# Softmax sums of the macaron block: their inverses stored to DRAM in the order of z, in 4-byte pieces

## The reference

```
x = x + 0.5 * ffn(layernorm(x))      # 8 experts, the best 2 of each token, hidden width 512
x = x + attention(layernorm(x))      # 16 heads of width 64, causal
x = x + 0.5 * ffn(layernorm(x))

attn = softmax(masked / sqrt(64)); z = attn @ v; out = sum over heads of W_O z
```

## Time and profile before

| What | Value |
|---|---|
| Time, median of 3 runs | 1082.57 us (1079.71 to 1084.22) |
| Time of the profiled execution | 1080.58 us |
| Its span in the profile | 1078.8 us |
| PE busy | 970.3 us (90%) |
| DVE busy | 809.0 us (75%) |
| ACT busy | 698.7 us (65%) |
| POOL busy | 288.1 us (27%) |
| Granted TensorE clock, mean | 0.971 |

### The profile page before, as it was taken

The page is one execution under the profiler, slowest core; times in us unless marked ns, Lnnn a source line. Parts: engine busy times, 40 slices in busy tenths (PEclk is TensorE's granted clock), DMA queues, the critical chain, the costliest instruction groups (busy, mean ns, idle before and its releaser), DMA issues.

```text
span 1078.8 us, 24385 instructions
## 1 busy us (share of the span) xinstructions
PE 970.3 (90%) x7643; PEld 818.8 (76%) x7643; DVE 809.0 (75%) x3154; ACT 698.7 (65%) x1966; POOL 288.1 (27%) x329
## 2 busy tenths in 40 slices
PE   7316889987999999999999999999999998978993
PEld 6315889986777877877787787787787776978993
DVE  7513568875868878978978978978878886856786
ACT  2304657655787777778778778778777775645672
POOL 5472320115101101231231231130100103455554
PEclk9999889988999999999999999999999999989997
DMA  9314545631112102112212212211111123435575
GB/s 251 105 58 120 158 157 158 197 92 49 36 31 41 34 28 41 42 39 43 44 40 41 46 38 41 45 38 31 48 27 31 47 58 118 139 106 168 166 239 167
DMA packets 92767, 90.57 MB, mean 84 GB/s; under 512 B 30304, under 2 KB 68352, under 8 KB 92640
## 3 DMA queue, kind: packets, MB, share of 16 engines
q1 hardware_dynamic: 79440, 68.13, 22.7%
q0 software_dynamic: 8640, 18.76, 6.6%
q10 hardware_dynamic: 4560, 2.12, 0.7%
HBM read 64.75 MB, written 24.22 MB: 82 GB/s over the span
## 4 chain that ended last, share of the span: by engine, by line
PE 82%; another core or an unknown queue 5%; DVE 4%; issue 4%; ACT 2%; DMA 1%; SPq 0%; POOL 0%; POOLq 0%; DVEq 0%; ACTq 0%
PE psum L2153 14%; PE psum L2164 13%; PE psum L2110 12%; PE psum L2016 10%; PE psum L1969 7%; PE psum L1967 7%; PE psum L1968 7%; PE psum L2172 6%; PE psum L1979 2%; PE psum L1880 2%; PE psum L1989 1%; PE psum L1873 1%; ACT arena L796 0%; DVE y_sb L1528 0%
## 5 line engine op out<-in xcount | busy, mean ns | idle before, releaser
L903 ACT ACTIVATE arena<-arena,neg_max 128x512 f32<-128x512 f32 (+3 forms) x512 | 281.5, 558 | 1.6 <-issue 1.6
L1638 DVE CUSTOM_DVE_ANT_0 arena<-psum,causal 128x512 f32<-128x512 f32 (+3 forms) x512 | 217.1, 481 | 4.9 <-PE psum L2110 4.9
L911 ACT ACTIVATE arena<-psum 128x512 f32<-128x512 f32 x192 | 103.9, 597 | 156.6 <-PE psum L2153 153.2
L2016 PE MATMUL psum<-w_sb,arena 128*128 x1192 | 156.7, 284 | 10.1 <-issue 8.5
L857 ACT ACTIVATE arena<-psum,b_t 128x256 f32<-128x256 f32 (+1 forms) x332 | 124.6, 455 | 62.8 <-PE psum L1969 33.8
L2153 PE MATMUL psum<-ident,arena 128*128 128x128 f32 x1280 | 158.0, 277 | 4.4 <-issue 1.8
L2016 PEld LDWEIGHTS psum<-w_sb,arena 128*128 128x128 f32 x1192 | 148.4, 200 | 13.2 <-issue 12.9
L2164 PE MATMUL psum<-arena 128*64 128x512 f32 (+3 forms) x1024 | 152.0, 439 | 0.7 <-DVE arena L1651 0.7
L2153 PEld LDWEIGHTS psum<-ident,arena 128*128 128x128 f32 x1280 | 143.3, 143 | 10.7 <-ACT arena L911 3.8
L725 POOL DMA_INDIRECT arena<-y_tiles,y_at x64 | 61.1, 955 | 314.2 <-PE psum L2110 203.5
L2164 PEld LDWEIGHTS psum<-arena 128*64 128x64 f32 x1024 | 68.0, 136 | 83.9 <-issue 74.1
(11 more groups left out here) (304 smaller groups left out, 1935.7 us busy)
## 6 DMA issues: line engine op xcount, KB each, us to landing
w_raw<-in_L_ffn_W_dram SPq DMA_DIRECT2D x66, 256.0 KB
arena<-inv_dram SPq DMA_DIRECT2D x128, 128.0 KB
xg<-x_slots SPq DMA_DIRECT2D x55, 144.0 KB
arena<-in_L_ffn_W_dram SPq DMA_DIRECT2D x17, 256.0 KB
arena<-y_rows SPq DMA_DIRECT2D x16, 256.0 KB, 3.5
y_tiles<-y_sb SPq DMA_DIRECT2D x27, 128.0 KB, 1.7
x_slots<-blank SPq DMA_DIRECT2D x18, 144.0 KB
out_dram<-xs ACTq DMA_DIRECT2D x8, 256.0 KB
```

The lines of the kernel that those rows point to most:

```text
L903: ins = act.activation(prob_tile(i, h, t), prob_tile(i, h, t), ACT.Exp, scale=-1.0, bias=neg_max[i % 2][:, h, t:t + 1], accum_out=row_sum[ ...
L911: act.activation(four_turned(g), turned_bank(i, g), ACT.Copy).then_inc(pt_act, 1)
L1638: ins = dve.tensor_tensor_reduce(out=prob_tile(i, h, t), in0=score_tile(t, h), in1=causal[:, SEQ - (t + 1) * P:SEQ], scale=-1.0, scalar=-2 ...
L2016: ins = pe.matmul(Y_BANKS[side(f, n)][:, r * D:(r + 1) * D], h_t[side(f, n)][:, k, r * P:(r + 1) * P], w2_sb[:, bass.ds(e * (CHUNKS * D) + ...
```

## The change

The scratch in DRAM is laid out in the order of the queries, [h, t * 128 + q], where it was [h, q, t]. The store reads the same 8 numbers of each partition. Before, the 4 numbers of a head lay side by side in DRAM, so a store was 256 pieces of 16 bytes; now neighbours in a partition go 512 bytes apart, so it is 1024 pieces of 4 bytes. The two loads still read 2 KB into each of 64 partitions. The multiplication on VectorE then reads all three operands in order, where it read `inv_bc` with a step of 16 bytes.

```diff
@@ the tiles
-        inv_bc = [lot(SEQ).rearrange("p (q t) -> p q t", t=QT) for i in range(2)]
+        inv_bc = [lot(SEQ) for i in range(2)]
...
-        w1_raw += [inv_bc[i].rearrange("p q t -> p (q t)") for i in range(2)]
+        w1_raw += inv_bc
...
-        inv_dram = nc.dram_tensor("inv_dram", [2, 2, P, QT], fp32).ap()
+        inv_dram = nc.dram_tensor("inv_dram", [2, 2, SEQ], fp32).ap()
@@ SyncE, spread_sums
-                sp.dma_start(inv_dram[par].rearrange("h q t -> q h t"), inv_sum[par][:, :, :]).then_inc(inv_stored, 16)
+                sp.dma_start(inv_dram[par].rearrange("h (t q) -> q h t", t=QT), inv_sum[par][:, :, :], allow_slow_non_contiguous=True).then_inc(inv_stored, 16)
                 sp.wait_ge(inv_stored, 16 * (i + 1))
                 for h in range(2):
                     sp.dma_start(
-                        inv_bc[par][h * DH:(h + 1) * DH, :, :],
-                        inv_dram[par, h].rearrange("q (o t) -> o q t", o=1).broadcast_to([DH, P, QT]),
+                        inv_bc[par][h * DH:(h + 1) * DH, :],
+                        inv_dram[par, h].rearrange("(o t) -> o t", o=1).broadcast_to([DH, SEQ]),
                     ).then_inc(inv_loaded[par], 16)
@@ VectorE, divide_by_sums
-                dve.tensor_tensor(z_sb.rearrange("p (t q) -> p t q", t=QT), RING_C.rearrange("p (t q) -> p t q", t=QT),
-                                  inv_bc[i % 2].rearrange("p q t -> p t q"), ALU.mult).then_inc(z_ready, 1)
+                dve.tensor_tensor(z_sb, RING_C, inv_bc[i % 2], ALU.mult).then_inc(z_ready, 1)
```

## The result

The changed kernel takes 1453.89 us (median, 1449.72 to 1454.65) against 1082.8 us before, a ratio of 1.342 [1.339, 1.346]: 371 us slower. The forecast was no visible change, 1082.2 us, with a range up to 1115; the result lies far above the range. Its profiled span is 1451.7 us.

What follows compares the result with a forecast made beforehand. TensorE was taken to bound the attention: -0.4 (last multiplication) - 0.5 (one wait) + 0.5 (late steps at the end) = -0.4 us, so 1080.2 profiled, 1082.2 as median; range 1077 to 1115.

Steps and rivals of the forecast that it cites:

- VectorE's 25 us: In the attention, 64 multiplications each 393 ns shorter save VectorE 25.2 us, nearly all beside TensorE's work.
- 682 ns for the multiplication: Multiplication on VectorE falls from 1075 to 682 ns, taken from the same operation with operands in order.
- 49152 packets more: Sign of being right: SyncE's queue carries 64 x 768 = 49152 packets more, 128592 in all.
- the rest is start and confirmation, which come once for each store: In the store, 256 pieces take about 0.25 us of one step's 1.8; the remainder does not grow with pieces.
- D: Extra time of each store with 1024 pieces instead of 256: taken as 0.75 us, bounded by 0 and 4.7.
- the far bound of 4.7: Store wholly proportional to its number of pieces: 4 x 1.56 = 6.2 us, so 4.7 us longer.
- The bound from the load of x: First load of x, 1024 pieces, landed 4.3 us after issue: store 2.7 or 1.8 us longer.
- the rival: In the attention, the store closes a loop and sets the step: slower, most of it below 1120 us, chance 0.28.
- The loop: Multiplication to next inverse, store, loads, next multiplication: 7.9 to 8.5 us + D, against a step of 10.05.
- The rival's own rule: From D = 1.5 to 2.1 us on, the loop sets the step; each further us costs 63 us.
- its far end: At D = 4.7 the loop is 12.6 to 13.2 us: +160 to +198 us, some 1260.
- 0 to 10 us: Cost claimed for the kernel when the store closes the loop at D = 2.1.

Runs made afterwards that it cites:

- the multiplication alone: Kernel before with only the multiplication changed, reading the inverses as they lie in memory, store still 256 pieces of 16 bytes: 1082.71 us, ratio 1.0005.

## Why the prediction was wrong

- **TensorE bounds the attention, and VectorE's 25 us are covered**: right, shown by the multiplication alone (ratio 1.0005).
- **682 ns for the multiplication**: right, 692. The rise from 682 to 1075 is a factor of 1.6, not the doubling that the prediction calls it. That the step of 16 bytes was the reason is now supported by the kernel with a step of 8, 691 ns; it agrees with the 16-byte lines in the Trainium skill, "SBUF — State Buffer", section "Door 1: The DMA port swizzle".
- **49152 packets more, sent within 1 us**: right, 128592 on the queue, and the traffic of a store ends by 648.5 of an issue at 646.54.
- **The step that failed is the sentence "the rest is start and confirmation, which come once for each store"**. From it came D = 0.75 us. Measured, D is 556.1 / 61 + 0.37 - 2.5 = 7.0 us, more than the far bound of 4.7. The confirmation came once, but it was not of fixed length: it depends on where the pieces land. In the changed kernel the pieces were gone 2 us after the issue and the confirmation came 6.4 us later. Four or more 64-byte lines of DRAM, each filled by 16 writes, took 7 to 14 us on an idle core. The bound from the load of x says nothing about that, since a load writes to SBUF (2.3 us for 1024 pieces) and a line is read once; and "4 x 1.56" supposed that the pieces, not their neighbours, set the cost. The prediction does say that no row shows how DRAM takes neighbouring writes, and then leaves that to the rival and gives it no room in D; that neighbours come from different engines of the transfer, as it adds, no run shows.
- **The loop**: right as a mechanism, and it decided. z to inverse 1.8 us, release 0.23, store 9.5, loads to z 15.87 - 1.8 - 0.23 - 9.5 = 4.3 us (3.4 to 4.0 were forecast). (15.87 - 10.05) x 63 = 367 us of the 373 us by which the span grew. The rival's own rule, 63 us for each us of D beyond 1.5 to 2.1, gives 309 to 347 us at D = 7.0. The rival had the right path and sign and was given 0.28, but even its far end, some 1260 us, lay below 1454. Its margin was too wide: 7.0 - (15.87 - 10.05) = 1.2 us, for 1.5 to 2.1. And its "0 to 10 us" at D = 2.1 is a slip: its loop is 10.0 to 10.6 us there, so 0 to 35 us.
- **The Trainium skill's rule against strided last dimensions** ("DMA: Bandwidth & Descriptors", section "Rules for kernel authors") was cited and then outweighed by a row that showed only the sending. Even the 19 times of "VectorE: DVE Perf Modes", section "The three transpose paths", taken at its word (D = 4.5) would have come nearer than the rows did; the same figure, turned into 1.5 ns a piece, had given D = 1.2. Neither holds the reason that the runs show: 1024 strided pieces are fast when they lie apart.
- **The clock**: the lower granted clock in the attention was named as a sign. It follows TensorE's idle stretches (0.50 from 644.5 to 651 us, after no matmul at all between 641.5 and 645). The chain above holds no matmul, and at that clock TensorE still stands idle 3.9 us a step before z, so the slower clock is mostly hidden; a run that shows its share apart was not made.

## What to carry to other kernels

A store that other work waits for has two durations: the traffic of its pieces, which the profile shows, and the silence from the last piece to the semaphore, which here depended on where the pieces land and was 6.4 us behind 1 us of traffic. Before many small pieces go to DRAM, look whether many of them fill the same 64-byte line, and time that one store alone in a loop of store and wait; a run of eleven such forms took 470 us here and would have settled this case. And where a path of transfers closes a loop beside a busy engine, its margin (here 1.1 to 1.5 us in a step of 10.05, by the kernels with two stores and with pieces of 8 bytes) is what to compare a change with, not the engine's share of the span.

## What the runs showed of the hardware that was not expected

- 256 pieces of 4 bytes side by side in DRAM land in 8.8 us, 1024 in 10.2, and 1024 pieces 512 bytes apart in 2.9. Pieces of 8 bytes side by side take 3.4 us, of 16 bytes 1.5.
- 16 pieces of 4 bytes in each of 128 lines of 64 bytes take 13.7 us, one piece in each 1.4.
- VectorE's product of a PSUM and an SBUF operand, 128 x 512 fp32, takes 691 ns at a step of 8 bytes in SBUF and 1075 at 16.
